# Local attention of a two-layer transformer kernel: output projection for two units at once, placed ahead of the scores; bias of padded keys by products of full height

## The reference, cut to what matters

```python
x = x + _L0_xattn_ref(_layernorm(x), ctx_4096, Wq, bq, Wk, bk, Wv, bv, Wo, bo)

q = Wq @ x + bq ; k = Wk @ cond + bk ; v = Wv @ cond + bv     # 64 channels -> 64 channels
k, v = pad(k, 8, 7), pad(v, 8, 7)                             # padded with zeros, after the bias
dots = einsum('bhdt,bhdtw->bhtw', q, k_win) * hd ** -0.5      # 16 keys for each position
out = einsum('bhtw,bhdtw->bhdt', softmax(dots), v_win)
return Wo @ out + bo
```

## Time and profile before

| | |
|---|---|
| time, median of 3 runs | 1135.47 us (1133.59 to 1136.64) |
| time of the profiled execution | 1131.74 us |
| its span, first to last instruction | 1129.9 us |
| mean granted TensorE clock | 0.964 of full speed |
| local attention ends (last L599) | 174.15 us after the span's start |

### The profile page before, as it was taken

The page is one execution under the profiler, slowest core; times in us unless marked ns, Lnnn a source line. Parts: engine busy times, 40 slices in busy tenths (PEclk is TensorE's granted clock), DMA queues, the critical chain, the costliest instruction groups (busy, mean ns, idle before and its releaser), DMA issues. The chain is left out here.

```text
span 1129.9 us, 24015 instructions
## 1 busy us (share of the span) xinstructions
PE 1043.6 (92%) x9170; PEld 867.2 (77%) x9170; DVE 660.0 (58%) x1357; ACT 352.3 (31%) x826; POOL 515.3 (46%) x594
## 2 busy tenths in 40 slices
PE   7899988999999879999999999999999999755993
PEld 3677777888887678888888888888888888534783
DVE  4799874544544675656565556656555565850424
ACT  3677744222222232222222222222222321211331
POOL 3555531422223355445454554444554542337755
PEclk9799999999999889999999999999999999986997
DMA  7100006656350021111011111111011100036768
GB/s 236 24 4 4 4 3 177 207 196 224 139 207 28 29 66 38 47 29 48 29 29 48 32 41 41 29 48 29 28 48 34 33 10 1 1 122 210 250 217 269
DMA packets 51806, 92.07 MB, mean 81 GB/s; under 512 B 10748, under 2 KB 24316, under 8 KB 51260
## 3 DMA queue, kind: packets, MB, share of 16 engines
q1 hardware_dynamic: 42108, 69.13, 19.2%
q10 hardware_dynamic: 6624, 12.06, 3.1%
q0 software_dynamic: 2976, 9.44, 2.5%
HBM read 77.25 MB, written 36.18 MB: 100 GB/s over the span
## 5 line engine op out<-in xcount | busy, mean ns | idle before, releaser
L121 PE MATMUL PS<-NTh,W 128*128 128x256 f32 (+2 forms) x688 | 216.5, 315 | 0.0
L122 PE MATMUL PS<-NTl,W 128*128 128x256 f32 (+2 forms) x688 | 214.0, 311 | 0.0
L123 PE MATMUL PS<-NTh,W 128*128 128x256 f32 (+2 forms) x688 | 213.9, 311 | 0.0
L122 PEld LDWEIGHTS PS<-NTl,W 128*128 128x128 f32 (+1 forms) x688 | 131.2, 191 | 6.9
L123 PEld LDWEIGHTS PS<-NTh,W 128*128 128x128 f32 (+1 forms) x688 | 129.4, 188 | 8.4
L121 PEld LDWEIGHTS PS<-NTh,W 128*128 128x128 f32 (+1 forms) x688 | 129.7, 189 | 7.1
L1501 POOL TENSOR_TENSOR W<-ca_raw,W 128x512 fp32r<-128x512 f32 x64 | 82.6, 1292 | 112.2 <-ACT W L1354 112.2
L1439 DVE TENSOR_REDUCE ca_su<-room 128x4 f32<-128x256 f32 x64 | 26.8, 419 | 154.5 <-ACT room L1368 154.5
L1468 DVE TENSOR_TENSOR room<-PS,ca_sinT 64x512 f32<-64x512 f32 (+1 forms) x192 | 115.0, 599 | 2.6
L121 PE MATMUL PS<-W,ca_aTh 128*128 128x512 f32 x256 | 106.9, 418 | 3.2 <-DVE X L1456 3.1
L122 PE MATMUL PS<-W,ca_aTh 128*128 128x512 f32 x256 | 101.3, 396 | 0.0
(11 more groups left out here) (253 smaller groups left out, 2350.3 us busy)
## 6 DMA issues: line engine op xcount, KB each, us to landing
ca_raw<-in_L_Wq SPq DMA_DIRECT2D x32, 256.0 KB, 2.8
ca_raw<-in_L_Wo SPq DMA_DIRECT2D x32, 256.0 KB, 2.6
rf_raw<-in_experts SPq DMA_DIRECT2D x28, 256.0 KB, 4.3
room<-slots ACTq DMA_DIRECT2D x23, 256.0 KB, 3.4
outs<-room ACTq DMA_DIRECT2D x23, 256.0 KB, 3.7
outs<-blank SPq DMA_DIRECT2D x11, 512.0 KB, 9.1
room<-in_L_Wg SPq DMA_DIRECT2D x10, 256.0 KB, 2.8
room<-in_L_Wu SPq DMA_DIRECT2D x10, 256.0 KB, 3.0
```

The lines of the kernel that those rows point to most:

```text
L121: nc.tensor.matmul(out, l_hi, r_hi, start=first, stop=False)
L122: nc.tensor.matmul(out, l_hi, r_lo, start=False, stop=False)
L123: return nc.tensor.matmul(out, l_lo, r_hi, start=False, stop=last)
```

## The change

The output projection (`AO`) is done for two units at once: the moving operand is 256 columns instead of 128, and the addition to `x` is one instruction of 128 x 256 instead of two of 128 x 128. `pair_due(n)` says in which step: in every odd step from 7 to 31 for the pair (n - 7) // 2, then in steps 32, 34 and 36. The tile lies in the free half of score bank 0 (in the last steps in bank 6, as before). On TensorE it moves from behind the scores to ahead of the band mask and the scores; on VectorE the addition moves ahead of the maximum, and the statistics at q = 1 move from their place around the reciprocal to the end of the step. The product for the bias of padded keys has 128 rows of which 127 are zero, instead of one row.

```diff
+    PAIR_T, PAIRS = 2 * UNIT_T, UNITS // 2
+    def pair_due(n):
+        if n < UNITS:
+            return (n - 7) // 2 if n >= 7 and n % 2 == 1 else None
+        return (n - 6) // 2 if n % 2 == 0 and n - 6 < UNITS else None
...
-        less = sb("wa_less", [1, 2, P])
-        bv_row = sb("wa_bv_row", [1, P])
+        less = sb("wa_less", [P, 2, P])
+        bv_row = sb("wa_bv_row", [P, P])
...
-        oh = sb("wa_oh", [P, 2, HH, UNIT_T])
+        oh = sb("wa_oh", [P, 2, HH, PAIR_T])
...
-        AO = sh.PS[:, 6, 256:256 + UNIT_T]
+        AO = [sh.PS[:, 0, 256:256 + PAIR_T], sh.PS[:, 6, 256:256 + PAIR_T]]
...
@@ TensorE, step(n): ahead of the values
-                        if not isinstance(n, int) or m >= 3:
-                            pe.wait_ge(S["x_added"], m - 2)
+                        if n >= UNITS and pair_due(n - 1) is not None:
+                            pe.wait_ge(S["x_added"], pair_due(n - 1) + 1)
...
@@ behind the values
+                    p = pair_due(n)
+                    if p is not None:
+                        pe.wait_ge(S["oh_copied"], 2 * p + 2)
+                        if n >= UNITS:
+                            pe.wait_ge(S["vt_copied"], min(n - 2, UNITS))
+                        if p >= 1:
+                            pe.wait_ge(S["x_added"], p)
+                        else:
+                            pe.wait_ge(S["wo_ready"], 1)
+                        for h in range(HH):
+                            last = nc.tensor.matmul(AO[n >= UNITS], wo[:, h, :], oh[:, p % 2, h, :], start=h == 0, stop=h == HH - 1)
+                        last.then_inc(S["ao_mm"], 1)
                     if live(n, UNITS):
+                        if pair_due(n - 1) is not None:
+                            pe.wait_ge(S["x_added"], pair_due(n - 1) + 1)
                         for b2 in range(2):
                             nc.tensor.matmul(SC[:, b2, :], exact_id[:], exact_band[:], start=True, stop=False)
...
@@ behind the scores
-                    m = n - 5
-                    if live(m, UNITS):
...
-                        for h in range(HH):
-                            last = nc.tensor.matmul(AO, wo[:, h, :], oh[:, (u - 5) % 2, h, :], start=h == 0, stop=h == HH - 1)
-                        last.then_inc(S["ao_mm"], 1)
...
@@ VectorE, step(n)
-                    if q == 1 and live(t - 2, TT - 1):
-                        vec.wait_ge(S["x_added"], 4 * t - 4)
                     m, w = n - 2, (u - 2) % 4
                     if live(m, UNITS):
                         vec.wait_ge(S["exped"], m + 1)
                         nc.vector.reduce_sum(su[:, w, :], sm[:, w, :, :], AX_X).then_inc(S["summed"], 1)
-                        if q == 1 and live(t - 2, TT - 1):
-                            norm.count(vec, t - 2, slot)
-                            norm.await_count(vec, t - 2)
                         vec.wait_ge(S["summed"], m + 1)
                         nc.vector.reciprocal(rc[:, w, :], su[:, w, :]).then_inc(S["recip"], 1)
-                    if q == 1 and live(t - 2, TT - 1):
-                        norm.aggregate(vec, t - 2, slot)
...
                         nc.vector.transpose(sm[:, u % 4, :, :].rearrange("p (b x) k -> p b (x k)", b=2),
                                             SC).then_inc(S["keyed"], 1)
+                    p = pair_due(n)
+                    if p is not None:
+                        vec.wait_ge(S["ao_mm"], p + 1)
+                        x = sh.X[:, p // 2, p % 2 * PAIR_T:(p % 2 + 1) * PAIR_T]
+                        nc.vector.scalar_tensor_tensor(x, AO[n >= UNITS], bias[:, 3:4], x, ALU.add, ALU.add).then_inc(S["x_added"], 1)
+                    if live(n, UNITS):
                         vec.wait_ge(S["keyed"], n + 1)
                         nc.vector.reduce_max(mx[:, u % 4, :], sm[:, u % 4, :, :], AX_X).then_inc(S["maxed"], 1)
+                    if q == 1 and live(t - 2, TT - 1):
+                        vec.wait_ge(S["x_added"], 2 * t - 2)
+                        norm.count(vec, t - 2, slot)
+                        norm.await_count(vec, t - 2)
+                        norm.aggregate(vec, t - 2, slot)
                     if q == 3 and live(t - 2, TT - 1):
                         norm.low(vec, t - 2, PJ)
-
-                    m, w = n - 5, (u - 5) % 4
-                    if live(m, UNITS):
-                        vec.wait_ge(S["ao_mm"], m + 1)
...
```

More of the change, by code:

```diff
@@ L337, in window_attention @@
         names = ("const_loaded loaded zeroed padded ct_tr ct_hi ct_lo w_tr w_ready wo_ready stats aggr veps power_set rstd normed "
-                 "q_mm k_mm q_biased q_ready k_ready edges bv_loaded sc_mm masks_ready keyed maxed subbed exped summed recip probs "
+                 "q_mm k_mm q_biased q_ready k_ready edges bv_zeroed bv_loaded sc_mm masks_ready keyed maxed subbed exped summed recip probs "
                  "rowed vt_mm vt_copied oh_mm oh_copied ao_mm x_added").split()
@@ L354, in _ @@
                 load(sh.CTX, "ctx", ctx_loaded, *LOADS[0])
+                sp.wait_ge(S["bv_zeroed"], 1)
                 for b2 in range(2):
-                    sp.dma_start(bv_row[:, b2 * SEQ:(b2 + 1) * SEQ], d["L0_bv"].rearrange("(a c) -> a c", a=1)
+                    sp.dma_start(bv_row[0:1, b2 * SEQ:(b2 + 1) * SEQ], d["L0_bv"].rearrange("(a c) -> a c", a=1)
                                  ).then_inc(S["bv_loaded"], 16)
@@ L502, in step @@
                             pe.wait_ge(S["ct_lo"], c - 1)
+                        if c == 0:
+                            pe.wait_ge(S["x_added"], pair_due(UNITS - 1) + 1)
                         for k in range(EC):
@@ L625, in _ @@
                 nc.gpsimd.memset(wT[:], 0.0).then_inc(S["zeroed"], 1)
+                nc.gpsimd.memset(bv_row[:], 0.0).then_inc(S["bv_zeroed"], 1)
                 nc.gpsimd.memset(blank[:], 0.0).then_inc(S["zeroed"], 1)
@@ L632, in _ @@
                 gp.wait_ge(S["padded"], 4)
-                nc.gpsimd.memset(less[:, 0, 0:PAD], -1.0).then_inc(S["padded"], 1)
-                nc.gpsimd.memset(less[:, 1, P - PAD:], -1.0).then_inc(S["padded"], 1)
+                nc.gpsimd.memset(less[0:1, 0, 0:PAD], -1.0).then_inc(S["padded"], 1)
+                nc.gpsimd.memset(less[0:1, 1, P - PAD:], -1.0).then_inc(S["padded"], 1)
                 gp.wait_ge(S["padded"], 6)
@@ L728, in step @@
                         act.wait_ge(S["oh_mm"], m + 1)
-                        if not isinstance(n, int) or m >= 2:
-                            act.wait_ge(S["ao_mm"], m - 1)
-                        nc.scalar.activation(oh[:, u % 2, :, :].rearrange("p h (i x) -> p i h x", i=4),
+                        if m >= 4:
+                            act.wait_ge(S["ao_mm"], (m - 4) // 2 + 1)
+                        nc.scalar.activation(oh[:, m // 2 % 2, :, m % 2 * UNIT_T:(m % 2 + 1) * UNIT_T].rearrange("p h (i x) -> p i h x", i=4),
                                              OH.rearrange("p i (h x) -> p i h x", h=HH), ACT.Identity,
```

4 lines of the change are left out of this document (removed).

## The result

| kernel | median us | lowest to highest | runs |
|---|---|---|---|
| before | 1134.53 | 1132.11 to 1136.64 | 4 |
| changed | 1154.39 | 1153.78 to 1155.89 | 4 |

The ratio is 1.0181, 95% interval [1.0159, 1.0203]: slower by 19.9 us. The profiled execution took 1154.26 us with a span of 1152.5 (before 1131.74 and 1129.9). The output projection's last addition ends at 194.99 us instead of 174.15, so 20.84 of the span's 22.6 us arise in the local attention. The other 1.8 lie behind it; no run here assigns them. What follows the attention is the same code in all nine kernels here, and it took from 953.7 to 960.2 us in their profiled executions.

A forecast was written before the change was run, and what follows sets the result against it. TensorE was taken to set the pace, 16.81 us busy of 17.26 per tile. Attention +13.4 us, +16.9 together, on the profiled 1131.7 gave 1148.6; from the 1135.5 median basis, 1152 us, range 1142 to 1161.

The forecast's parts named there:

- q = 1 to 2: Interval between score transpositions along VectorE alone, with statistics, GpSimd's root and norm uncovered: 5.94 us.
- q = 2 to 3: Interval between score transpositions, with values, bias, pair and band on TensorE and VectorE's work hidden: 4.51 us.
- q = 3 to 0: Interval between score transpositions through VectorE's low part, then TensorE's query projection to scores: 4.84 us, before 4.62.
- q = 0 to 1: Interval between score transpositions along TensorE alone, VectorE waiting about 2 us of it: 4.87 us.
- The pair's price: Output projection of two units on TensorE: eight passes of 256 columns, 1.78 us; other bound 1.88.
- The bias product: TensorE, two full-height steps 0.48 us instead of 0.73: -0.25 for each of two products per tile.
- the rival by which the bias edit does nothing: Rival: 0.25 us per bias product is not saved, +1.5 us, inside the range; no separate chance given.
- The whole stage without the clock: Local attention: steady tiles +14.5, their end -0.3, steps 28 to 31 +2.2, tile 1 -1.5, steps 32 to 36 -1.5: +13.4 us.
- The clock: TensorE's granted clock in the attention: one fall of 3.5 us counted; up to three falls, 10.5, at the high end.
- TensorE's work decides: Rival: VectorE runs far enough ahead, tile about 16.2 us, -9 in all: 1126; chance of faster 0.08.
- 1170: Rival: the clock falls in every tile, 13.4 + 6 x 3.5 = 34 us; chance 0.08.
- Same: Rival: chain covered, L222 short, query projection released earlier, some 2.5 of 2.9 us per tile don't come: 1134; chance 0.04.

The follow-up runs named there:

- runs 2: Kernel before with only the statistics moved to the end of step q = 1, single projections kept: 1144.63 us, ratio 1.0102.
- run 4: Changed kernel with the norm moved behind the transposition of the probabilities in q = 2, late statistics kept: 1139.43 us, ratio to before 1.0048.
- run 1: Kernel before with only the bias product made 128 rows high: 1129.87 us, ratio 0.9961.
- run 5: Changed kernel with six unused products of 256 columns per tile around the norm's transposition on TensorE: 1146.94 us, ratio to before 1.0116.
- run 3: Changed kernel with the pair behind the scores in even steps and the statistics in their old place: 1133.65 us, ratio to before 0.9993.
- run 6: Kernel before with full-height bias, GpSimd's subtraction waiting in q = 2 and q = 3 until VectorE's norm ends: 1127.45 us, ratio 0.9935.

## Why the prediction was right, point by point

**Order, not work.** The interval between hand-overs of the one score tile decides, and its four lengths came out as worked out from the rows of before:

| interval | predicted | measured |
|---|---|---|
| q = 1 to 2 | 5.94 | 5.98 |
| q = 2 to 3 | 4.51 | 4.46 |
| q = 3 to 0 | 4.84 | 4.85 |
| q = 0 to 1 | 4.87 | 4.87 |
| tile | 20.16 | 20.16 |

TensorE stands still 4.73 us per tile (predicted 4.65). The chain from L198 to L222 took 1.76 us as it did at the seam, and the wait for the root 0.67 where the prediction said some 0.7. That it is this chain was shown by runs 2 (chain without the pair: 5.74) and 4 (pair without the open chain: 4.53). In the kernel before, four instructions stand between L210 and L222 (L580, L587, L590, L599 in the list), not six; they take the 2.45 us from 93.14 to 95.59, and the sum doesn't use their number.

**The pair's price was too high**, 1.78 predicted and 1.54 measured, and the sum hid it: in q = 2 to 3 the answer to the transposition took 0.16 us instead of 0.10, the three products ahead of the pair 0.75 instead of 0.72, band to scores 0.51 instead of 0.41. In q = 0 to 1 the pair's 0.24 is made up in the same way, by 0.11 at the band, 0.09 at the values and smaller ones. That these two intervals came out to 0.05 us and to nothing is thus partly luck; in the other two each term was near.

**The bias product** follows the row: the two steps, to it and from it, take 0.52 us (109.56 to 110.08) or 0.36 (103.93 to 104.29) in the changed kernel (predicted 0.48), against 0.73 with one row. The loads themselves took 184 ns in the median with one row and 192 with 128 (first before, then run 1; shortest, median and longest in ns):

```profile
L446 PEld LDWEIGHTS PS<-wa_bv_row,wa_less x32: 181/184/333, 29.4 to 165.2; 1*128 1x128 f32 x32
L447 PEld LDWEIGHTS PS<-wa_bv_row,wa_less x32: 192/192/333, 28.2 to 161.7; 128*128 128x128 f32 x32
```

So the load with one row is hardly shorter, but the time until the next product starts is longer, and the rival by which the bias edit does nothing didn't hold: run 1 shows the edit to be worth 4.7 us.

**The whole stage without the clock** was +13.4 and measured +11.8 (run 5). The transpositions of the scores in before and in run 5 show which terms were off (times in us):

| part | before | run 5 | difference | predicted |
|---|---|---|---|---|
| first transposition to that of step 8 | 33.33 | 31.37 | -2.0 | -1.5 |
| step 8 to 28 | 85.73 | 99.96 | +14.2 | +14.2 |
| step 28 to 31 | 12.47 | 14.76 | +2.3 | +2.2 |
| step 31 to the end | 20.69 | 17.93 | -2.8 | -1.5 |

The steady tiles came as worked out; at both ends more was saved than the prediction had. Part of it is the bias edit, which it didn't count there: alone it saves 1.0 us ahead of step 8 (run 1).

**The clock was the mis-sized term.** The prediction counted one fall of 3.5 us over six tiles; there were four falls, 9.5 us together. That is near the high end it kept (10.5, three falls). The 3.5 was the author's estimate and no run shows it: the four falls cost 1.6 to 2.8 us each. Three of them lie in the interval that was to pay for it, q = 2 to 3, and one in q = 3 to 0. The falls came with the idle time in the tile: with six more products in it the granted clock was 1.00 from 49 to 189 us (run 5), and with the norm covered one fall was left, 0.53 from 71 to 74 us (run 4). Why the tile at 102.70 keeps its clock with the same waits as one that falls is open.

**Terms that partly cancel.** The order was 1.6 us below its term and the clock 6 above, and the first transposition came 0.45 us earlier: the stage lost 20.84 us instead of 16.9. With the 1.8 us behind it, the profiled execution came 5.7 above the 1148.6. The median came out only 2.4 above the forecast, because the forecast had added 3.7 for the step from a profiled execution to a median, and for the changed kernel that step is 0.1. This nearness is luck.

**One premise failed:** "So TensorE sets the pace with 0.45 us of idle time". In the kernel before three of the four intervals end with VectorE not waiting at all, at 4.21 or 4.22 us each (85.15 and 98.20 in the earlier trace rows, and this one): its own instructions fill them, and TensorE is merely busy meanwhile.

```profile
93.98 0.72 DVE L587 STREAM_TRANSPOSE wa_sm<-PS 128x512 f32<-128x512 f32 x1
```

Run 1 took work from TensorE and left the steady tile at 17.17; run 6 took time from VectorE and it fell to 16.49. The busy share of 16.81 in 17.26 us misled. The forecast didn't rest on it, because the intervals were worked out engine by engine; the rival "TensorE's work decides" did. That TensorE also bounds what follows the attention, as the prediction says, was read from busy time too, and no run tests it.

**Rivals.** The clock fell in some tiles, not in every one (1170 would have needed that). "Same" needed the chain covered; run 4 covers it, and this takes off 15 of the 20 us, but not all: 1139.43 us, still above 1134.58.

## What to carry to other kernels

Where two engines hand one buffer to and fro, cost an edit by the intervals between hand-overs, each along the engine that ends last in it, and not by the sum of work; a saving on an engine that waits anyway is returned as waiting (0.85 us instead of 0.37 ahead of the query projection in run 1). When a batch is formed, look at what needs its result: here the pair's sum came late enough to strip a chain over three engines of its cover, and the pair saved nothing to pay for it, even where the chain stayed covered (run 3). And when an edit makes TensorE idle, add the clock as a term of its own: here it cost 9.5 us beside the 11.8 of the order.

## What the runs showed of the hardware

- A norm of 128 x 512 on VectorE takes 0.54 us when no subtraction of GpSimd has begun (run 6), and 1.23 when one has started 0.10 us earlier. In the kernel before it began at 95.59 beside this instruction, which ends at 96.54, and ended 0.28 us after it:

```profile
95.49 1.05 POOL L663 TENSOR_TENSOR wa_sm<-wa_sm,wa_mx 128x512 f32<-128x512 f32 x1 [0.79 <-DVE wa_mx L590]
110.15 1.28 POOL L673 TENSOR_TENSOR wa_sm<-wa_sm,wa_mx 128x512 f32<-128x512 f32 x1 [0.83 <-DVE wa_mx L602]
```

The second line, of the changed kernel, shows the reverse: there the norm L542 began 0.16 us earlier (109.99), took 0.54, and the subtraction took 1.28 instead of 1.05. Where GpSimd was first, which happens in six of the nine kernels, the norm ended 0.27 to 0.29 us after GpSimd's instruction, whether it took 0.55 us (run 4) or 1.26. By what means one instruction holds up the other no trace shows. Making GpSimd wait was worth 2.4 us here, although GpSimd then starts later.
- Falls of the clock cost the changed kernel 9.5 us, nearly as much as the new order that brought them (11.8), and useless products gave 7.5 of the total back.
- A bias product of one row between full-height products costs TensorE 0.73 us for two steps, full height 0.36 or 0.52: a smaller operand was the dearer one, and its load took 184 ns in the median against 192. Why was not measured.
